# Every fourth unit's turned attention weights taken from PSUM by ScalarE, as 255 less them

## The reference, cut to what matters

```python
def _fq(x, delta, zp, n_bits):
    xi = _round_ste(x / delta) + zp
    xq = jnp.clip(xi, 0.0, 2.0 ** n_bits - 1.0)
    return (xq - zp) * delta

def _attn(x, ctx, wq, wk, wv, wo, bo, dq, dk, dv, dw):
    ...
    sim = jnp.einsum('bhid,bhjd->bhij', _fq(q, dq, 128.0, 8), _fq(k, dk, 128.0, 8)) * SCALE
    attn = jax.nn.softmax(sim, axis=-1)
    out = jnp.einsum('bhij,bhjd->bhid', _fq(attn, dw, 0.0, 8), _fq(v, dv, 128.0, 8))
    out = out.transpose(0, 2, 1, 3).reshape(b, n, D)
    return out @ wo + bo
```

## Time and profile before

| | |
|---|---|
| median of 3 runs | 3306.69 us (3295.16 to 3310.97) |
| the profiled execution, its own time | 3299.79 us |
| its span, first to last instruction | 3298.0 us |
| mean granted TensorE clock | 0.94 |
| busy: TensorE, VectorE, ScalarE, GpSimd | 2906.8, 2119.9, 1499.5, 1773.5 us |

### The profile page before, as it was taken

One profiled execution on the slowest core, in us unless ns is written; L12 is line 12 of the kernel. 1 busy time (PEld: TensorE's weight loads), 2 busy tenths in 40 slices (PEclk: granted clock), 3 DMA queues, 4 the chain that ended last, 5 costly groups with the idle time before them and its releaser, 6 DMA issues.

```text
span 3298.0 us, 50801 instructions
## 1 busy us (share of the span) xinstructions
PE 2906.8 (88%) x19712; PEld 2120.9 (64%) x19712; DVE 2119.9 (64%) x3543; ACT 1499.5 (45%) x2178; POOL 1773.5 (54%) x1698
## 2 busy tenths in 40 slices
PE   7676786897889889899889899899988899899998
PEld 6565555556667656667677656666777756666777
DVE  4457695783665586696565587687565588688521
ACT  5332462663423364474334275375333266276321
POOL 3555583884545185485355186386364277377321
PEclk9888657999999999899999999999999999999999
DMA  8754103334543314324352412334353322232444
GB/s 273 239 190 148 57 9 115 122 129 185 171 160 119 134 40 154 122 98 160 118 184 90 157 68 104 122 116 153 130 195 105 144 81 95 92 141 91 166 166 153
DMA packets 199758, 436.40 MB, mean 132 GB/s; under 512 B 94944, under 2 KB 103392, under 8 KB 182368
## 3 DMA queue, kind: packets, MB, share of 16 engines
q1 hardware_dynamic: 199520, 433.15, 36.9%
HBM read 363.38 MB, written 65.54 MB: 130 GB/s over the span
## 4 chain that ended last, share of the span: by engine, by line
PE 55%; POOL 18%; DVE 11%; ACT 6%; issue 6%; DMA 2%; SPq 1%; POOLq 0%; DVEq 0%; ACTq 0%
PE psum L1729 16%; PE psum L1730 14%; PE psum L1731 14%; POOL w1b L1005 7%; PE psum L2025 3%; POOL rec L1000 3%; DVE e L1616 2%; PE psum L2013 2%; ACT psum L1198 2%; PE psum L2039 1%; POOL u_lo L1024 1%; ACT e L1303 1%; POOL den L998 1%; POOL fw_lo L1012 1%; POOL x L921 1%
## 5 line engine op out<-in xcount | busy, mean ns | idle before, releaser
L1303 ACT ACTIVATE e<-e,nb 128x1024 f32<-128x1024 f32 x512 | 588.3, 1149 | 328.9 <-DVE e L1616 326.3
L1616 DVE TENSOR_SCALAR_CACHE_REDUCE e<-psum,nscale 128x1024 f32<-128x1024 f32 x512 | 652.4, 1278 | 76.0 <-POOL w1b L1005 59.7
L1005 POOL TENSOR_SCALAR w1b<-e,rec 128x1024 f16<-128x1024 f32 x512 | 574.7, 1122 | 91.6 <-POOL rec L1000 57.4
L1729 PE MATMUL psum<-h_hi,fw_hi 128*128 128x512 f32 x1024 | 456.0, 445 | 30.9 <-DVE h_lo L1390 10.0
L2025 PE MATMUL psum<-ident,w1b 128*128 128x128 f16 x4096 | 344.6, 232 | 81.9 <-POOL w1b L1005 51.5
L2025 PEld LDWEIGHTS psum<-ident,w1b 128*128 128x128 f16 x4096 | 253.8, 103 | 250.0 <-issue 132.7
L1629 DVE TENSOR_SCALAR w1T<-psum 128x1024 bf16<-128x1024 f16 x512 | 352.3, 688 | 93.5 <-PE psum L2025 90.2
L1730 PE MATMUL psum<-h_lo,fw_hi 128*128 128x512 f32 x1024 | 409.0, 399 | 0.0
L1731 PE MATMUL psum<-h_hi,fw_lo 128*128 128x512 f32 x1024 | 407.9, 398 | 0.0
L915 POOL TENSOR_TENSOR rstd<-ve,mhalf 128x1 f32<-128x1 f32 x128 | 86.9, 679 | 475.1 <-DVE ve L1496 475.1
L1488 DVE TENSOR_TENSOR x<-psum,x 128x512 f32<-128x512 f32 x224 | 152.2, 684 | 229.5 <-PE psum L1731 228.7
(11 more groups left out here) (182 smaller groups left out, 6065.2 us busy)
## 6 DMA issues: line engine op xcount, KB each, us to landing
fw_hi<-pieces SPq DMA_DIRECT2D x168, 512.0 KB, 3.3
fw_lo<-pieces SPq DMA_DIRECT2D x168, 512.0 KB, 4.3
w_hi<-kept SPq DMA_DIRECT2D x45, 1024.0 KB, 5.1
w_lo<-kept SPq DMA_DIRECT2D x45, 1024.0 KB, 7.4
mixed<-mixed SPq DMA_DIRECT2D x32, 1024.0 KB, 5.1
fbias<-in_fside_Bx16xSxS SPq DMA_DIRECT2D x64, 256.0 KB, 3.1
unsplit<-in_L_xattn_ff_w SPq DMA_DIRECT2D x24, 512.0 KB, 5.2
pieces<-fw_hi SPq DMA_DIRECT2D x24, 512.0 KB, 2.6
```

The source lines that it names most:

```text
L1005: pool.tensor_scalar(w1b[u % NH][:], e1[u % NE][:], rec1[:, u % 8:u % 8 + 1], HALF, ALU.mult, ALU.add).then_inc(w1_ready.sem, 1)
L1303: act.activation(e1[s % NE][:], e1[s % NE][:], ACT.Exp, bias=nb1[:, s % NE:s % NE + 1], scale=-1.0, accum_out=sum1[:, s % 8:s % 8 + 1]).th ...
L1616: emptied_bank(dve.tensor_scalar(e1[s % NE][:], psum[:, i:i + 2, :].rearrange("p i n -> p (i n)"), nscale[:, 0:1], LARGEST, ALU.mult, ALU.min,
L1729: pe.matmul(o, s_hi, m_hi, start=first, stop=False)
```

## The change

In every group the fourth unit (head 3, u % 4 == `TURNED_ROUND`) is now taken out of bank 4 by ScalarE instead of VectorE. ScalarE has Relu and no minimum, so it writes Relu((1024 + 255) - w1b), which is 255 less the clipped weight, to the same buffer. In slot s it does so for unit s - 5, ahead of the exponential of unit s. The value product of head 3 is then 255 x (sum of values) less what was wanted; a second product with the same stationary values, and a moving operand that is -255 in every column (`all_high`, one column read 128 times), is added after each of head 3's, and the sign of `unit_v` is turned for head 3's 32 partitions. The waits on the buffers' use go into a helper.

```diff
+TURNED_ROUND = 3
...
+        above = sb("above", [P, 1])
+        all_high = sb("all_high", [P, 2], BF16)
...
+        def wait_weights_used(eng, n, g):
+
+            if g % 4 == 3:
+                wait_filled(eng, ("a1", n, g // 4))
+            else:
+                eng.wait_ge(w1T_used.sem, w1T_used.at((n, g)))
...
             def self_attention(n):
 
                 for s in range(S_SLOTS):
+                    u = s - LAG_T
+                    if 0 <= u < UNITS and u % 4 == TURNED_ROUND:
+                        key = ("p1T", n, u)
+                        wait_filled(act, key)
+                        if u >= 8:
+                            wait_weights_used(act, n, u // 4 - 2)
+                        act.activation(w1T[u % 8][:].rearrange("p k q -> p (k q)"), bank(bank_of(key)).bitcast(FP16), ACT.Relu,
+                                       bias=above[:, 0:1], scale=-1.0).then_inc(emptied[bank_of(key)], 1)
                     if s < UNITS:
                         wait_emptied(act, ("s1", n, s))
...
+            dve.memset(above[:], HALF + W_HIGH)
+            dve.memset(all_high[:], -W_HIGH)
...
-                dve.tensor_tensor(unit_v[:, i:i + 1], dw, dv, ALU.mult)
+                link(dve.tensor_tensor(unit_v[:, i:i + 1], dw, dv, ALU.mult))
             landed()
+            rest = slice(DH * TURNED_ROUND, DH * TURNED_ROUND + DH)
+            dve.tensor_scalar(unit_v[rest, 0:1], unit_v[rest, 0:1], -1.0, None, ALU.mult)
...
-                    if 0 <= u < UNITS:
+                    if 0 <= u < UNITS and u % 4 != TURNED_ROUND:
...
-                                ins = pe.matmul(bank(5)[DH * h:DH * h + DH, t * P:t * P + P], v1[:, k, hd:hd + DH],
-                                                w1T[4 * (g % 2) + h][:, k, :], start=(k == 0), stop=(k == KEYT - 1))
+                                o = bank(5)[DH * h:DH * h + DH, t * P:t * P + P]
+                                last = k == KEYT - 1
+                                ins = pe.matmul(o, v1[:, k, hd:hd + DH], w1T[4 * (g % 2) + h][:, k, :], start=(k == 0),
+                                                stop=last and h != TURNED_ROUND)
+                                if h == TURNED_ROUND:
+                                    ins = pe.matmul(o, v1[:, k, hd:hd + DH], all_high[:, 0:1].broadcast_to((P, P)), start=False,
+                                                    stop=last)
```

More of the change, by code:

```diff
@@ L1623, in self_attention @@
                         if u % 4 == 0 and u >= 8:
-                            g = u // 4 - 2
-                            if g % 4 == 3:
-                                wait_filled(dve, ("a1", n, g // 4))
-                            else:
-                                dve.wait_ge(w1T_used.sem, w1T_used.at((n, g)))
+                            wait_weights_used(dve, n, u // 4 - 2)
                         emptied_bank(dve.tensor_scalar(w1T[u % 8][:].rearrange("p k q -> p (k q)"),
```

## The result

The changed kernel takes 3397.3 us (median of 4 runs, 3380.4 to 3402.9); the kernel before took 3305.0 in the same comparison. The ratio is 1.0282, 95% interval 1.0262 to 1.0301: slower by 92 us. The forecast was 3372, its range ended at 3395. The sign and the main mechanisms were right; the size was too small by a quarter. The profiled execution has a span of 3399.8 us against 3298.0 before, 101.8 more, and the traces are compared on that.

What follows compares the result with a forecast made beforehand. TensorE time is paid in full in the fourth, sixth and eighth stage; the third, fifth and seventh have little room; the first is a serial loop. 45 + 9 + 10 + 6 + 2 = 72 us on 3299.8 gives 3372 us, range 3330 to 3395.

Steps and rivals of the forecast that it cites:

- The products in the fourth, sixth and eighth stage, 7.2 us each: Value products on TensorE: each added product costs a 0.057 us step, 0.23 us per half group, 7.2 us per stage.
- The late Relu there, 7.8 us: Fourth, sixth, eighth stage: TensorE waits for Relus delayed on ScalarE, 2.8 and 2.4 us behind gelus, about 7.8 per stage.
- the sum of that stage, 7.2 + 7.8: Fourth, sixth and eighth stage: added products plus waits for late Relus, 3 x (7.2 + 7.8) = 45 us.
- The third, fifth and seventh stage, 3 us each: TensorE becomes the slowest of three engines, but only just: +3 us each, 9 in all, bounds -2 and +6 each.
- 1 to 3 us more behind gelus: Third, fifth and seventh stage: the extra beside TensorE's 8.1 us per group, within the +3 taken for each stage.
- The first stage, 10, the second, 6: First: +13 products, +7 Relu waits, against VectorE's 10, gives +10 us; second: 7.2 + 8, more than half covered by GpSimd, +6.
- The clock rises: Rival, first stage: products raise the clock, the stage runs at GpSimd's pace, 22 us below the forecast's figure; 3350, chance 0.06.
- a clock above 0.6: First stage: a granted clock above 0.6, against 0.51 before, was named as a sign that the forecast is wrong.
- VectorE's 10 us there: First stage: gain from taking a quarter of the turns off VectorE and its shorter cycle in other slots, 10 us.
- Only the products count: Rival: ScalarE runs ahead of need, so Relu is never late; 32 us slower, 3332, chance 0.12.
- ScalarE's lateness feeds back: Rival: GpSimd waits for late exponentials at some 21 gelus, about 1.8 us each, 38 us more; 3410, chance 0.12.
- VectorE was the bound: Rival, faster: first stage gains 7 us, third, fifth and seventh 8 each, as TensorE's work fits into waits; 3269, chance 0.06.

Runs made afterwards that it cites:

- products_only: Changed kernel with VectorE turning all units again and the 1024 added products kept, with zeros in place of -255; 3340.2 us, ratio 1.0117.
- products_rotated: Against products_only: as many added products, the round's one going to head k mod 4 behind the other four; 3312.4 us, ratio 1.0042.
- scalar_only: Changed kernel without the added products; ScalarE takes every fourth unit with Identity and bias -1024, no clip at 255; 3351.8 us, ratio 1.0154.
- relief_only: Kernel before, with VectorE turning only 128 of 1024 columns of every fourth unit from the eighth on, nothing given to other engines; 3298.8 us, ratio 0.9993.
- folded_1: Against round_1: the 1024 products replaced by 32 two-column products at each stage's start, added as bias of the attention output's scaling; 3354.8 us, ratio 1.0164.
- stall_idle: Kernel before, with TensorE waiting for a later exponential ahead of units 8 and 28 in the second, fourth, sixth and eighth stage; 3325.4 us, ratio 1.0073.
- round_1: Changed kernel with TURNED_ROUND 1 in place of 3, so ScalarE takes units 4g+1; all products stay; 3360.6 us, ratio 1.0183.
- folded_late: Against folded_1: VectorE takes unit 57 or 29 of each stage, and the 32 small products move from slot 0 to slot 3; 3316.7 us, ratio 1.0055.

## Why the prediction was wrong, and where it was right

**The products in the fourth, sixth and eighth stage, 7.2 us each: right.** products_only grew them by 6.4, 8.3 and 6.1. Between unit 0 and 63 it is 5.9, 5.5 and 5.6: most half groups take 0.22 to 0.24 us more, as reckoned (0.23), and what is missing to 7.2 fell mostly into waits that TensorE had before at units 7 and 59. products_rotated confirmed why they cost it.

**The late Relu there, 7.8 us: right as a wait.** The slots of the sixth stage give 8.1, at the places named (two behind a gelu, some smaller); one more of 1.6, at unit 59, was not among the long ones.

**What failed is the sum of that stage, 7.2 + 7.8.** It ends a wait where TensorE starts again, and puts what follows at nothing. In the sixth stage 5.9 us more were lost behind the waits, at half clock. The earlier trace rows had the sign of it: a clock of 0.51 in the stage with idle time and 0.97 in those without. I used that row for the first stage, as a rival in which the clock rises, and not for the fourth, where my own 2.8 us waits could lower it. The term measured 20.0, 22.4 and 22.3, 64.7 in place of 45, some 5 of it by the half clock at which the sixth and the eighth were entered.

**The third, fifth and seventh stage, 3 us each: too small**, 22.7 in place of 9. Products alone are 3.0 to 3.2 there, all that had been put down for products and Relu together; the sum's own 8.1 against 8.0 per group makes 1.6 for a stage. So less of the added work was covered than reckoned. The "1 to 3 us more behind gelus" was 4 in the fifth, again with the clock: units 31, 32 and 33 took 1.4, 1.7 and 1.1 us more than with products alone. This is unit 31's Relu behind the one gelu of the fifth stage:

```profile
2013.19 0.62 PE L2043 MATMUL psum<-ident,w1b 128*128 128x128 f16 x8
2017.16 1.01 PE L2043 MATMUL psum<-ident,w1b 128*128 128x128 f16 x8 [2.13 <-ACT w1T L1317]
```

Eight transposes take 1.01 us behind that wait and 0.62 ahead of it.

**The first stage, 10, the second, 6: measured 7.1 and 4.3**, but the first came about differently. The rival *The clock rises* was half true, and the prediction's own sign of being wrong, a clock above 0.6, came. Its price did not: 71 slots at GpSimd's 7.48 per group are 133 us, 18 below the 151 of that sum and not 22. With the products the clock rose to 0.66, and in products_only to 0.71, where the stage grew by 0.5 us in place of the 13 that the products were to cost; scalar_only stayed at 0.53 and grew by 3.7. VectorE's 10 us there were too much: relief_only gave 3.3, with seven eighths of the work of 14 of those 16 turns left out.

*Only the products count* fell with scalar_only. *ScalarE's lateness feeds back* gave the nearest time, 3410, and by luck: with the few units behind a gelu taken away, five in six of the Relus cost 7 us beside the products, though every gelu is still there, and the account of the sixth stage leaves no room for it. Its price was miscounted too. The self-attention stages hold 15 gelus (three in each stage with 112 quarter steps, one in each with 72), not 21, which makes 27 us in place of 38. *VectorE was the bound* fell with relief_only. The last unit's +2 was not measured by itself.

## What to carry to other kernels

Where TensorE is the bound, ask of work moved to another engine not how much time that engine has, but what stands ahead of it in its order at each place where TensorE waits; the 128 Relus cost 50 us by themselves, and 7 beside the products once the 20 close behind a gelu were taken away. Count a TensorE wait of about 2 us or more, such as these, once for its length and then again for the half clock that may follow, which cost 1.5 to 2.9 us behind each wait where it came in the sixth stage. And put a small step so that the bank it writes is free, or all that is queued behind it waits too: one slot number was worth 14 us.

## What was not expected of the hardware

Two waits of the same length, 2.66 us, at the same place of two stages of one execution were followed by half clock once and by full clock once. The length of the wait does not settle it. Counted over the fourth, sixth and eighth stage, and within 2 us of the wait's end, half clock followed all nine long waits of the changed kernel (1.9 to 2.3 us) and all three of folded_1 (2.4), four of six in stall_idle (2.7), five of nine in scalar_only (2.4 to 2.5) and none of three in round_1 (2.0). What else decides it is open.

And 32 products of two columns each, in 32 columns of the array, took 1.01 us together at half clock and 0.95 at full clock, 0.03 us for each either way, so the array's clock did not set their time. folded_late, at full clock:

```profile
2148.75 0.95 PE L2050 MATMUL psum<-all_high,v 128*32 128x2 bf16 x32
```
